# One column of a gathered block fetched row by row by SyncE and ScalarE instead of by GpSimd

## What is computed

```python
# layer 0, attention: k, q, v by node type, typed per edge
ke, qe, ve = (k[src], q[dst], v[src])
a = (kw * qw).sum(-1) * rel_pri[:, etype].T / sqrt_d
h = segment_sum(m * softmax_over_dst(a)[:, :, None], dst)
# layer 1, gated attention
z_src = z[src]; pw = pre_w * v[src]
# layer 2: a polynomial of the edge weights times g[cols] (not touched here)
# layer 3: three convolutions
def conv(h, W, b):
    m = concatenate([h[dst], h[src], edge_attr], axis=1) @ W + b
    return segment_sum(m, dst, num_segments=n_nodes)
```

## Time and profile before

| | us |
|---|---|
| median of 2 runs without the profiler | 11907.03 (11906.45 to 11907.6) |
| span of the profiled execution | 13242.4 |
| POOL busy in that span | 9106.3 (69%) |
| DVE, ACT busy | 4015.6 (30%), 3476.7 (26%) |
| PE busy | 1352.0 (10%) |
| POOL busy in the gathers of line 864 | 6549.8 + 1644.1 |

### The profile page before, as it was taken

One profiled execution on the slowest core, in us unless ns is written; L12 is line 12 of the kernel. 1 busy time (PEld: TensorE's weight loads), 2 busy tenths in 40 slices (PEclk: granted clock), 3 DMA queues, 4 the chain that ended last, 5 costly groups with the idle time before them and its releaser, 6 DMA issues. The chain is left out here.

```text
span 13242.4 us, 37433 instructions
## 1 busy us (share of the span) xinstructions
PE 1352.0 (10%) x6735; PEld 1005.3 (8%) x6735; DVE 4015.6 (30%) x5472; ACT 3476.7 (26%) x4561; POOL 9106.3 (69%) x8728
## 2 busy tenths in 40 slices
PE   5200000020000000395000000200000000000000
PEld 3100000010000000273000000200000000000000
DVE  2255555544445544695111111011111101111110
ACT  2333223312222222375232222122211212221121
POOL 3677777767777776402777777577777767777776
PEclk7655555555555555697555555555555555555555
DMA  7333333313333333001222222111111111111111
GB/s 277 133 97 97 98 95 95 100 34 90 98 95 94 94 99 81 14 1 32 61 58 61 58 58 60 40 50 46 49 46 46 49 39 50 46 49 46 46 49 42
DMA packets 404823, 919.05 MB, mean 69 GB/s; under 512 B 171046, under 2 KB 195277, under 8 KB 389496
## 3 DMA queue, kind: packets, MB, share of 16 engines
q0 software_dynamic: 278944, 386.91, 13.3%
q1 hardware_dynamic: 121832, 529.42, 10.9%
q10 hardware_dynamic: 3824, 0.50, 0.0%
HBM read 456.45 MB, written 459.77 MB: 69 GB/s over the span
## 5 line engine op out<-in xcount | busy, mean ns | idle before, releaser
L864 POOL DMA_INDIRECT arena<-tab,src x6256 | 6549.8, 1047 | 2894.4 <-issue 2101.0
L2244 DVE TENSOR_TENSOR_SCAN arena<-cv_keep,arena 128x768 f32<-128x768 f32 (+1 forms) x476 | 752.0, 1627 | 5757.2 <-issue 4526.3
L864 POOL DMA_INDIRECT arena<-tab,spread x1564 | 1644.1, 1051 | 518.5 <-issue 518.5
L2106 ACT COPY arena<-arena 128x1472 f32<-128x1472 f32 x204 | 545.3, 2673 | 3003.9 <-DMA arena<-tab,src 3003.9
L2111 ACT COPY arena<-arena 128x1472 f32<-128x1472 f32 (+1 forms) x204 | 588.3, 2884 | 551.8 <-DVE arena L2244 431.2
L1089 PE MATMUL e_t<-ident,arena 128*68 128x128 f32 (+1 forms) x2 | 0.8, 397 | 4433.5 <-PEq L1433 2223.3
L2168 PE MATMUL cv_t<-ident,arena 128*81 128x128 f32 (+1 forms) x294 | 137.9, 469 | 2917.7 <-ACT arena L2118 1528.3
L2105 ACT COPY arena<-arena 128x368 f32<-128x368 f32 x68 | 55.3, 813 | 1353.7 <-issue 1325.1
L2182 PE MATMUL cv_t<-ident,arena 128*64 128x128 f32 (+1 forms) x3 | 1.3, 425 | 3391.1 <-ACT arena L2111 3391.1
L951 ACT ACTIVATE ae_prob<-arena 128x92 f32<-128x92 f32 x68 | 17.1, 251 | 1228.8 <-remote 1152.7
L1089 PEld LDWEIGHTS e_t<-ident,arena 128*68 128x68 f32 (+1 forms) x2 | 0.3, 134 | 4433.9 <-issue 4433.9
(11 more groups left out here) (370 smaller groups left out, 6943.0 us busy)
## 6 DMA issues: line engine op xcount, KB each, us to landing
rows<-arena SPq DMA_DIRECT2D x68, 1506.5 KB
arena<-tab,src POOLq DMA_INDIRECT x6256
rows3b<-arena SPq DMA_DIRECT2D x136, 736.0 KB
rows<-arena SPq DMA_DIRECT2D x68, 920.0 KB
rows<-arena SPq DMA_DIRECT2D x68, 828.0 KB
tab<-arena SPq DMA_DIRECT2D x49, 1024.0 KB
q_start<-arena SPq DMA_DIRECT2D x32, 1564.0 KB
arena<-q_start SPq DMA_DIRECT2D x68, 736.0 KB
```

The costliest lines, as they stand in the source:

```text
L864: pool.indirect_dma_start(out=rows[b][:, j, :], out_offset=None, in_=table, in_offset=bass.IndirectOffsetOnAxis(ap=idx[:, at:at + 1].bitca ...
L2106: nc.scalar.copy(chain[:, 0:D, 1:C1], rin[b].rearrange("p j f -> p f j")).then_inc(s_in, 1)
L2244: ins = v.tensor_tensor_scan(out=part, data0=keep[:, 0:(f1 - f0) * C1], data1=part, initial=0.0, op0=ALU.mult, op1=ALU.add)
```

## The change

For an "aided" block the last of its 23 columns is not gathered by POOL. Its 128 rows are fetched by 128 single-row DMAs, whose source address is a byte offset in a register. Blocks from 64 on are never aided. In the two attention passes every second block is aided, by SP alone; in the convolutions every block below 64 is, 80 of its rows by SP and 48 by ACT. The registers come 16 at a time out of lists in SBUF, which DVE prepares once in the first phase by three multiplications and three transposes. The buffers in the attention passes grow from two to three, and the consumers also wait on one of four new semaphores.

```diff
+LISTED = 64
+LOADS = 16
+ATT_SHARE = (1, 2)
+CONV_SHARE = (1, 1)
+SP_ROWS = 80
...
+def aided(c, share):
+    num, den = share
+    return int(c < LISTED and (c + 1) * num // den > c * num // den)
...
+def fetch_rows(nc, eng, engine, row_list, table, c, chunks, dest, signal):
+    size = dest.shape[-1] * 4
+    flat = table.rearrange("n f -> (n f)").bitcast(U8)
+    for k in chunks:
+        p = k * LOADS
+        at = p % 32 + c // 32 * 32
+        _, values = nc.values_load_multi_w_load_instructions(
+            row_list[p // 32 * 32 + c % 32:p // 32 * 32 + c % 32 + 1, at:at + LOADS], engines=[engine], min_val=0,
...
+        for x, value in enumerate(values):
+            eng.dma_start(dest[p + x:p + x + 1, C - 1, :].bitcast(U8), flat[bass.ds(value, size)].unsqueeze(0))\
+               .then_inc(signal, 16)
...
-        b = c % 2
-        wait(pool, s_rows, c - 1)
-        for j in range(C):
+        b = c % ring
+        wait(pool, s_rows, c - ring + 1)
+        for j in range(C - aided(c, share)):
...
# first pass, SP, ahead of the store of the block before
+                for later in (0, 1):
+                    if aided(c + later, ATT_SHARE):
+                        wait(sp, s_wtd, c + later - 2)
+                        chunks = range(0, P // LOADS // 2) if later else range(P // LOADS // 2 if c else 0, P // LOADS)
+                        fetch_rows(nc, sp, mybir.EngineType.SP, g.lists[:, 0, :], g.tab0, c + later, chunks,
+                                   kvr[(c + later) % 3], s_side[side_of(c + later, ATT_SHARE)[0]])
...
# second pass, SP, ahead of the store of the block
+                for later in (1, 2) if c else (0, 1, 2):
...
# convolutions, SP
+            early, late = range(0, SP_ROWS // LOADS // 2), range(SP_ROWS // LOADS // 2, SP_ROWS // LOADS)
+            for c in range(2):
+                side_rows(sp, mybir.EngineType.SP, c, range(0, SP_ROWS // LOADS))
             for c in range(NC):
                 wait(sp, s_in, c + 1)
                 if k == 0 and c + 2 < NC:
                     load_attrs(c + 2)
+                side_rows(sp, mybir.EngineType.SP, c + 2, early)
                 wait(sp, s_copied, c + 1)
                 sp.dma_start(dest[:, c * C:c * C + C, :], rows).then_inc(s_st, 16)
+                side_rows(sp, mybir.EngineType.SP, c + 2, late)
...
# convolutions, ACT
+            of_act = range(SP_ROWS // LOADS, P // LOADS)
             scale(0)
+            for c in range(2):
+                side_rows(act, mybir.EngineType.Activation, c, of_act)
             for c in range(NC):
                 take(c)
...
                 give(c)
+                if len(of_act):
+                    act.wait_ge(s_in, c + 1)
+                    side_rows(act, mybir.EngineType.Activation, c + 2, of_act)
```

More of the change, by code:

```diff
@@ L26 @@
 U32 = mybir.dt.uint32
+U8 = mybir.dt.uint8
 P = 128
@@ L134, in alloc @@
     g.spread = sb("spread", [P, J])
+    g.lists = sb("lists", [P, 3, LISTED], I32)
     g.first = sb("first", [P, 1], I32)
@@ L281, in first_phase @@
     sem = lambda n: new_sem(nc, ctx, "fp_" + n)
+    s_listed = sem("listed")
     s_pad, s_din, s_xin, s_ein, s_w, s_wlate, s_wconv, s_zero = map(sem, (
@@ L364, in first_phase @@
     src, idx8 = g.src[:, :], g.spread[:, :].bitcast(I32)
+    scaled = g.spread_poly[:, 0:3 * LISTED].bitcast(I32).rearrange("p (a b) -> p a b", b=LISTED)
     mean, var, rstd, ends, start, has = (g.small[:, k, :] for k in (0, 1, 2, 3, 6, 7))
@@ L793, in _ @@
             v.tensor_tensor(g.keep[:, 1:J], dst[:, 1:J], dst[:, 0:J - 1], ALU.is_equal).then_inc(s_all, 1)
-            v.scalar_tensor_tensor(out=idx8, in0=src, scalar=float(ET), in1=idx8, op0=ALU.mult, op1=ALU.add)
+            v.scalar_tensor_tensor(out=idx8, in0=src, scalar=float(ET), in1=idx8, op0=ALU.mult, op1=ALU.add)\
+             .then_inc(s_listed, 1)
             dve.wait_ge(s_all, 1)
@@ L800, in _ @@
             v.tensor_scalar(g.allT[:, :], g.allT[:, :], f[:, 7:8], None, ALU.add).then_inc(s_all, 1)
+            dve.wait_ge(s_listed, 1)
+            for x, (of, width) in enumerate(((idx8, 2 * D), (src, G1), (src, D))):
+                column = of.rearrange("p (c j) -> p c j", j=C)[:, 0:LISTED, C - 1]
+                ins = v.tensor_scalar(scaled[:, x, :], column, 4.0 * width, None, ALU.mult)
+            ins.then_inc(s_listed, 1)
+            dve.wait_ge(s_listed, 2)
+            for x in range(3):
+                v.transpose(g.lists[:, x, :], scaled[:, x, :])
             with dve.Fori(3, MIDDLE) as i:
@@ L854, in _, with gathered, side_of, gather_columns @@
             v.tensor_copy(g.a2row[:, :], ps_w[:, 260:260 + D])
-def gather_columns(pool, table, idx, rows, s_gath, s_rows):
+def aided(c, share):
+    num, den = share
+    return int(c < LISTED and (c + 1) * num // den > c * num // den)
+def gathered(c, share, ring):
+    return 16 * sum(C - aided(x, share) for x in range(c % ring, c + 1, ring))
+def side_of(c, share):
+    n = sum(aided(x, share) for x in range(c))
+    return n % 4, (n // 4 + 1) * 16 * P
+def fetch_rows(nc, eng, engine, row_list, table, c, chunks, dest, signal):
[6 more added lines that the diff above has]
+            row_list[p // 32 * 32 + c % 32:p // 32 * 32 + c % 32 + 1, at:at + LOADS], engines=[engine], min_val=0,
+            max_val=(table.shape[0] - 1) * size,
+            skip_runtime_bounds_check_because="byte offsets of the rows that the indirect gathers use too")
+        for x, value in enumerate(values):
+            eng.dma_start(dest[p + x:p + x + 1, C - 1, :].bitcast(U8), flat[bass.ds(value, size)].unsqueeze(0))\
+               .then_inc(signal, 16)
+def gather_columns(pool, table, idx, rows, s_gath, s_rows, share):
+    ring = len(rows)
     for c in range(NC):
-        b = c % 2
-        wait(pool, s_rows, c - 1)
-        for j in range(C):
+        b = c % ring
+        wait(pool, s_rows, c - ring + 1)
+        for j in range(C - aided(c, share)):
             at = c * C + j
@@ L887, in attention_edges_phase @@
     s_qin, s_st, s_copied, s_chained, s_cm, s_qc = map(sem, ("q_in", "stored", "copied", "chained", "carried", "q_carried"))
-    s_gath = [pool_sem(g, f"gathered{b}") for b in range(2)]
+    s_gath = [pool_sem(g, f"gathered{b}") for b in range(3)]
+    s_side = [sem(f"side{n}") for n in range(4)]
     s_first = pool_sem(g, "first")
@@ L891, in attention_edges_phase @@
     at = 0
-    kvr = [None] * 2
-    for b in range(2):
+    kvr = [None] * 3
+    for b in range(3):
         kvr[b], at = view(g, at, C, 2 * D)
@@ L918, in _ @@
                 .then_inc(s_first, 16)
-            gather_columns(pool, g.tab0, g.spread, kvr, s_gath, s_wtd)
+            gather_columns(pool, g.tab0, g.spread, kvr, s_gath, s_wtd, ATT_SHARE)
         @block.sync
@@ L980, in _ @@
                 old = ends[:, 1 - b, :]
-                kv = kvr[b]
+                kv = kvr[c % 3]
                 if c:
@@ L994, in _ @@
                     if x == 0:
-                        dve.wait_ge(s_gath[b], (c // 2 + 1) * 16 * C)
+                        dve.wait_ge(s_gath[c % 3], gathered(c, ATT_SHARE, 3))
+                        if aided(c, ATT_SHARE):
+                            slot, full = side_of(c, ATT_SHARE)
+                            dve.wait_ge(s_side[slot], full)
                     dve.wait_ge(s_qe, n)
@@ L1413, in gated_edges_phase @@
     s_st, s_copied, s_chained, s_cm = map(sem, ("stored", "copied", "chained", "carried"))
-    s_gath = [pool_sem(g, f"gathered{b}") for b in range(2)]
+    s_gath = [pool_sem(g, f"gathered{b}") for b in range(3)]
+    s_side = [sem(f"side{n}") for n in range(4)]
     at = 0
-    rin = [None] * 2
-    for b in range(2):
+    rin = [None] * 3
+    for b in range(3):
         rin[b], at = view(g, at, C, G1)
@@ L1443, in _ @@
                 .then_inc(s_first, 16)
-            gather_columns(pool, g.tab1, g.src, rin, s_gath, s_wtd)
+            gather_columns(pool, g.tab1, g.src, rin, s_gath, s_wtd, ATT_SHARE)
         @block.sync
@@ L1450, in _ @@
             for c in range(NC):
+                for later in (1, 2) if c else (0, 1, 2):
+                    if aided(c + later, ATT_SHARE):
+                        wait(sp, s_wtd, c + later - 2)
+                        half = P // LOADS // 2
+                        chunks = range(0, half) if later == 2 else range(half if c else 0, 2 * half)
+                        fetch_rows(nc, sp, mybir.EngineType.SP, g.lists[:, 1, :], g.tab1, c + later, chunks,
+                                   rin[(c + later) % 3], s_side[side_of(c + later, ATT_SHARE)[0]])
                 wait(sp, s_copied, c + 1)
@@ L1493, in _ @@
                 b = c % 2
-                r, cols = rin[b], slice(c * C, c * C + C)
+                r, cols = rin[c % 3], slice(c * C, c * C + C)
                 old = ends[:, 1 - b, :]
@@ L2024, in conv_layer, with side_rows @@
         block = inner.enter_context(nc.Block())
+        def side_rows(eng, engine, c, chunks):
+            if aided(c, CONV_SHARE):
```

(9 more changed lines are left out.)

## The result

The changed kernel takes 13357.45 us (two runs, 13355.32 to 13359.58) against 11907.03: ratio 1.1219 [1.1197, 1.124], 12% slower. The prediction was 11625 us, range 11575 to 12450.

A forecast was written before the change was run, and what follows sets the result against it. The prediction took POOL's back-to-back gathers to bound every pass. Savings of 79 us in the attentions, 158 in two convolutions and 45 in the first, 282 in all off 11907, gave 11625 us, range 11575 to 12450.

The forecast's parts named there:

- What bounds the kernel: In all five passes POOL issues gather after gather without being held back by buffers; each gather less saves time.
- part 1: In aided blocks of all passes, 256 removed gathers at 1.235 us each take off 316 us if nobody else is slower.
- the late 1.397: POOL's us per gather after the first 201 us of a pass, against 1.248 before; taken as caused by profiling.
- the discount on r: On SP and ACT, 0.033 us taken off each row's two instructions as the profiler's, giving 0.295 instead of 0.36 us.
- r: Time SP or ACT needs to issue one single-row DMA with its MOVE and steps: 0.295 us used, 0.36 as traced.
- L: Time of one load of 16 registers on SP or ACT: 0.5 us used, 0.46 to 2.0 kept as bounds.
- Part 2: In the attention passes SP needs 21.8 to 25.9 us a block, under POOL's 27.2, so 79 us come off.
- the prediction's own formula: SP's block time above the old 28.4 us, times 128 and 64 convolution blocks and 128 attention blocks.
- The slow SP: In the convolutions, rows at the traced 0.36 us make SP the bound: 710 us lost, 79 won, 12540 us; chance 0.22.
- The serial loads: On SP, each load's sixteen values come one at a time, L 4.0 us: 16000 us in all; chance 0.05.
- The single engine: All single-row transfers use one DMA engine: convolutions take 20 us more per block at the higher price, 15700 us; chance 0.04.
- The price of a packet: In the single-engine rival, time per DMA packet: 0.10 us from POOL's queue or 0.19 from SP's; 256 packets a block.

The follow-up runs named there:

- without rows: The changed kernel with nothing fetching the 128 rows and no waits on them, shorter gathers kept: 11587.71 us.
- the half shares: The changed kernel with every second convolution block aided: 11787.9 us with no attention blocks aided, 11727.81 us with two attention blocks in five aided.
- fixed addresses: The changed kernel with the same 128 single-row DMAs per block at constant addresses, without register loads or registers in the DMA: 11851.28 us.
- two of three: The changed kernel with two of three convolution blocks and two of five attention blocks aided: 11745.13 us, ratio 0.9865.
- the attention kernel: The changed kernel with no convolution block aided and the attention passes left as changed: 11993.26 us.

## Why the prediction was wrong

**What bounds the kernel, and part 1, were right.** A removed gather brings 1.24 us as long as nobody else is late: 317 us of 316 without rows, and the half shares lose none of theirs. The price, 1.248 to 1.250 us where POOL does not wait, holds in all ten later profiles from the first gather of a pass to the last. So the late 1.397 of the earlier trace rows was rightly kept out of the sum; but "a thing of the profiled run" was wrong as a reason, since the later profiled runs don't have it.

**The step that failed first: the discount on r.** The prediction had 0.36 us for a row, read from SP, and took 0.033 off each of two instructions, because POOL's gathers could be worth that much less unprofiled. That transfer from POOL to SP had no row behind it, and there was nothing to take off: the nine spans of before show that the long trace was one execution out of line. In the trace of after, whose span is within 0.03% of the time, a row takes 0.343 us. The traced 0.36 was within 5%; 0.295 was 0.048 short, 3.8 us in a block of 80 rows.

**The larger one: the load, mis-sized.** L was taken as 0.5, bounds 0.46 to 2.0. It measures 1.27, inside the bounds, but the one load behind the block's store takes 2.70. Five of them are 4 x 1.27 + 2.70 = 7.8 us where the sum had 2.5: 5.3 us a block. Together with 0.1 more for the store, 26.5 + 3.8 + 5.3 + 0.1 = 35.7, SP's measured period. Either error alone takes the gain: with r = 0.295 and the measured loads SP needs 31.8 us, with the measured r and L = 0.5 it needs 30.3, both over the 28.4 that the prediction had for a block before.
The Trainium skill (Runtime: NRT & Kernel Launch, "Instruction fetch mechanics") asks some 200 ns for each register. Here, from lists in SBUF, it is 0.079 us for each of 16, or 0.059 beside a fixed 0.33 us: the rule rightly spoke against this change, and its size is two and a half times what was measured.

**Part 2, the attentions: same two errors.** 64 x 0.048 + (3 x 1.23 + 3.25 - 4 x 0.5) = 8.0 us more than 21.8 make 29.8, the period of 30.0 measured; the text had 25.9 at most, with L still at 0.5. The "over a microsecond left in each block" became 1.3 us too many against the old 28.7, and 79 us won became 86 lost. By the prediction's own formula with the measured terms, (35.7 - 28.7) x 128 + (36.9 - 28.7) x 64 + (30.0 - 28.7) x 128 = 1590 us, 13490; 1450 came. The formula lets POOL wait in every block, while the first wait comes after 28 blocks of the first pass and 36 of the second, and the second pass has no load of queries: its 64 blocks lost 7 us and not 83.

**The rivals.** The slow SP was the mechanism, as described: SP's block is the period, and POOL waits for `s_in`. Its price, 12540, kept L at 0.5; with the measured loads it is 28.8 + 7.8 + 0.4 = 37.0 us a block, which is over 13600 us and above the range. The prediction varied r with L at 0.5 (0.8 at most) and L with r at 0.295, so no case held r = 0.36 and L = 1.3 together, though each lay inside its own bounds. Two of its sums are off by themselves: at r = 0.325 its formula gives 12000 us and not 11880, and at L = 2.0 some 12980 and not 12900; neither changes the account. The serial loads did not come: 0.059 a register, not a trip for each. The single engine's price did not come either: transfers cost nothing in the attentions, and at fixed addresses, where 128 rows are fetched in each convolution block, at most (1987.8 - 1872.4) / 64 = 1.8 us a block against the 20 of that rival. The price of a packet can be read as the rival read it, from ACT's queue, which carried 3824 packets before and two more for each row now. The changed kernel, then the fixed addresses:

```profile
q10 hardware_dynamic: 22256, 2.89, 0.1%
...
q10 hardware_dynamic: 22256, 2.89, 1.1%
```

That is 0.1% x 16 x 13353.5 / 22256 = about 0.01 us, where the rival had 0.10 or 0.19: all 256 packets of a block would take one engine some 2.5 us. At fixed addresses the same packets took 0.09 us, near the rival's first price, and there POOL paused; whether the one brings the other is not shown. Which engine takes a row no run shows.

**The signs named ahead.** 22 gathers at 1.25 us: yes. L2106 (now L2190) waits for a DMA of SP: only once the store stands first; as the change has it, ACT waits one step earlier, for the store. SP's 80 rows equal the period: yes.

**Left open.** Why the load behind a block's store takes 2.70 or 3.25 us, and what holds POOL in every fifth block at fixed addresses and at two of three, were not tried.

## What to carry to other kernels

Work that is taken from the engine that bounds must be priced on the engine that receives it, against the receiver's time for one block, with all its unknown prices moved at once: here rows and loads were each varied alone, and the two together were the result. An engine that only issues has no busy time on the page, so its margin must be read as a period, from one of its instructions to the same one in the next block. And a share can be smaller than all: with one block of two in the convolutions and two of five in the attentions the same mechanism is worth 1.5%.

## What was not expected of the hardware

A load of 16 registers from SBUF takes 1.27 us, of 8 0.80, and with 16 registers 2.70 to 3.25 right behind the store of a block on the same queue. A single-row DMA holds SP 0.314 us at a fixed address and 0.343 at one in a register, on ACT 0.366. The gathers' slow rate after the first 201 us of each pass is in the one profiled execution of before alone, also for unchanged code: the unaided convolutions of the attention kernel have 1564 gathers in 1954 us, and nine more executions of the kernel before have spans of 11898 to 11906 us. Its cause stays unknown.
